# Copying the stack of keys by group of heads, in four bursts of small DMAs with a semaphore each

## The reference, cut to what matters

```python
q = split_heads(query @ Wq.T + bq)      # query: layernorm(x), 16 x 64 x 128
k = split_heads(key @ Wk.T + bk)        # key = value = ctx_1024, 16 x 1601 x 128
v = split_heads(value @ Wv.T + bv)
scores = jnp.einsum('bhqd,bhkd->bhqk', q, k) / np.sqrt(HEAD_DIM)
weights = jax.nn.softmax(scores, axis=-1)
out = jnp.einsum('bhqk,bhkd->bhqd', weights, v)
```

## Time and profile before

| | before |
|---|---|
| median of 3 runs | 583.64 us (582.66 to 584.8) |
| profiled execution, its own time | 585.52 us |
| span of the profiled execution | 583.7 us |
| PE busy | 526.1 us (90%) |
| DVE busy | 418.8 us (72%) |
| ACT busy | 380.7 us (65%) |
| POOL busy | 323.8 us (55%) |
| DMA queue of SP and ACT | 40.09 MB, 39.6% of 16 engines |
| mean granted TensorE clock | 0.970 |

### The profile page before, as it was taken

How to read it: one execution, slowest core, us unless ns; L and a number is a source line. 1 busy time by engine, 2 the same in 40 slices (tenths; PEclk the granted TensorE clock), 3 DMA queues, 4 the chain that set the end, 5 groups by cost and what they waited for, 6 DMA issues and landing times. The chain is left out here.

```text
span 583.7 us, 18814 instructions
## 1 busy us (share of the span) xinstructions
PE 526.1 (90%) x7882; PEld 341.0 (58%) x7882; DVE 418.8 (72%) x749; ACT 380.7 (65%) x704; POOL 323.8 (55%) x197
## 2 busy tenths in 40 slices
PE   2887999999998897999999898999889888999997
PEld 1634555665565464655655565665457565777776
DVE  6187888798797695887887887735887578555554
ACT  4874667677678575776777776976582616656562
POOL 1697968558558456576577279602200024676673
PEclk9887999999999998999999998999999979999999
DMA  7898664674574571754752946101100000000001
GB/s 214 127 131 132 140 104 91 97 117 89 86 116 89 87 108 39 117 105 71 123 106 35 144 84 110 40 2 53 47 2 2 2 1 1 2 2 0 0 0 37
DMA packets 16425, 41.62 MB, mean 71 GB/s; under 512 B 4006, under 2 KB 6830, under 8 KB 16234
## 3 DMA queue, kind: packets, MB, share of 16 engines
q1 hardware_dynamic: 15608, 40.09, 39.6%
q10 hardware_dynamic: 740, 0.42, 0.2%
HBM read 19.70 MB, written 0.52 MB: 35 GB/s over the span
## 5 line engine op out<-in xcount | busy, mean ns | idle before, releaser
L899 DVE TENSOR_REDUCE half_max<-wide 128x2 f32<-128x802 f32 x256 | 241.8, 988 | 57.5 <-PE wide L584 53.6
L824 ACT ACTIVATE probs<-score 128x512 f32<-128x512 f32 (+1 forms) x416 | 225.8, 596 | 75.4 <-PE score L635 75.0
L655 PE MATMUL sums<-probs,values 128*32 128x192 f32 (+3 forms) x3328 | 134.7, 282 | 5.9 <-issue 5.9
L655 PEld LDWEIGHTS sums<-probs,values 128*32 128x32 f32 (+1 forms) x3328 | 87.8, 110 | 60.0 <-issue 31.6
L584 PE MATMUL wide<-k_stack,q_cur 48*128 48x401 bf16 x512 | 88.9, 343 | 13.3 <-ACT k_full L806 6.2
L635 PE MATMUL score<-q_cur,k_stack 50*128 50x128 bf16 (+1 forms) x1664 | 83.4, 219 | 9.6 <-ACT probs L824 5.0
L415 POOL TENSOR_TENSOR ctx_hi<-ctx_in,one 128x1601 bf16<-128x1601 f32 x15 | 42.9, 2860 | 77.3 <-PE wide L506 68.5
L635 PEld LDWEIGHTS score<-q_cur,k_stack 50*128 50x128 bf16 (+1 forms) x1664 | 52.3, 95 | 35.0 <-ACT probs L824 11.3
L1892 POOL TENSOR_TENSOR hid_lo<-hid_e,hid_hi 114x512 bf16<-114x512 f32 x47 | 54.2, 1158 | 32.7 <-ACT hid_hi L1916 31.4
L427 POOL TENSOR_TENSOR k_hi<-k_full,one 128x1601 bf16<-128x1601 f32 x15 | 42.9, 2857 | 43.2 <-ACT k_full L806 34.7
L2027 DVE SCALAR_TENSOR_TENSOR hid_e<-gu,keep_bgu,gate 114x512 f32<-114x512 f32 x48 | 35.9, 750 | 38.5 <-ACT gate L1929 38.3
(11 more groups left out here) (327 smaller groups left out, 923.7 us busy)
## 6 DMA issues: line engine op xcount, KB each, us to landing
k_stack<-k_hi SPq DMA_DIRECT2D x64, 204.0 KB, 6.5
ctx_in<-in_ctx SPq DMA_DIRECT2D x56, 200.1 KB, 3.2
k_stack<-k_lo SPq DMA_DIRECT2D x32, 204.0 KB, 8.7
ctx_in<-in_wgu SPq DMA_DIRECT2D x16, 171.0 KB, 4.9
keep_w<-in_w SPq DMA_DIRECT2D x1, 1368.0 KB
ctx_in<-in_ctx SPq DMA_DIRECT2D x1, 800.5 KB, 8.3
keep_x<-in_x SPq DMA_DIRECT2D x1, 512.0 KB, 6.9
q_cur<-shift SPq DMA_DIRECT2D x30, 2.0 KB
```

Of the source, the lines that this page charges most:

```text
L655: last = pe.matmul(sums[32 * g:32 * g + 32, first * LQ:(first + heads) * LQ], values[0:m, n, k, VW * g + 2 * c:VW * g + 2 * c + 32], probs ...
L824: nc.scalar.activation(probs[0:m, step % NPROB, :].rearrange("r (g p c) -> r p g c", g=G, p=2)[:, p], score[0:m, (2 * step + p) % NSCORE, ...
L899: dve.tensor_reduce(half_max[:, b % 2, :, u // 4, u % 4], wide[:, w, :].rearrange("p (c k) -> p c k", c=2)[:, :, 0:CH], AX.X, ALU.max).the ...
```

## The change

The 6 DMAs of a stack become 24: each of them copies one group, so 16 rows of 1632 elements on both sides, with the source at every fourth partition of a half. For a batch the 6 DMAs of a group stand together. In bodies 1 to 13 the groups are begun at steps 0, 2, 5 and 7 (before: high parts at steps 0 and 1, low parts at step 3). In the prologue and in body 0 no step holds them back; for batch 0 the high parts of all groups come first. Each slot has four semaphores, one a group. PE waits for a group's semaphore at that group's first unit; POOL waits for all four.

```diff
-H_STEP, L_STEP, C_STEPS = 1, 3, (8, 9, 11, 12)
+G_STEPS, C_STEPS = (0, 2, 5, 7), (8, 9, 11, 12)
-        s_stack = [sem(f"s_stack{i}") for i in range(NSLOT)]
+        s_stack = [[sem(f"s_stack{i}_{g}") for g in range(G)] for i in range(NSLOT)]
-        def stacks_of(b):
-
-            return s_stack[b % NSLOT], N_STACK * (b // NSLOT + 1)
+        def stack_lies(e, b, g):
+
+            e.wait_ge(s_stack[b % NSLOT][g], N_STACK * (b // NSLOT + 1))
+            def stack_piece(n, g, term, keys):
+
+                for half in HALVES:
+                    at = half + PAIR * term
+                    sp.dma_start(k_stack[at:at + PAIR, n, g, :], keys[half + g:half + 64:G, :]).then_inc(s_stack[n][g], 16)
+
             def stack(i, b):
-                n, done = b % NSLOT, s_stack[b % NSLOT]
+                n = b % NSLOT
                 if b >= NSLOT:
                     sp.wait_ge(s_score, 2 * NK * (b - NSLOT + 1))
                 if b == 0:
                     sp.wait_ge(s_khi0, 2)
-                else:
-                    sp.wait_ge(s_khi, b)
-                for t in range(2):
-                    if t:
-                        at_step(i, H_STEP)
-                    for half in HALVES:
-                        at = half + PAIR * t
-                        sp.dma_start(k_stack[at:at + PAIR, n, :, :], k_hi[half:half + 64, :]).then_inc(done, 16)
-                at_step(i, L_STEP)
-                if b == 0:
+                    for g in range(G):
+                        for term in range(2):
+                            stack_piece(n, g, term, k_hi)
                     sp.wait_ge(s_klo0, 2)
-                else:
-                    sp.wait_ge(s_klo, b)
-                for half in HALVES:
-                    at = half + PAIR * 2
-                    sp.dma_start(k_stack[at:at + PAIR, n, :, :], k_lo[half:half + 64, :]).then_inc(done, 16)
+                    for g in range(G):
+                        stack_piece(n, g, 2, k_lo)
+                    return
+                sp.wait_ge(s_khi, b)
+                for g in range(G):
+                    if g:
+                        at_step(i, G_STEPS[g])
+                    for term in range(2):
+                        stack_piece(n, g, term, k_hi)
+                    if g == 0:
+                        sp.wait_ge(s_klo, b)
+                    stack_piece(n, g, 2, k_lo)
...
-                pool.wait_ge(*stacks_of(b - 1))
+                for g in range(G):
+                    stack_lies(pool, b - 1, g)
...
+                if part == 0:
+                    stack_lies(pe, b, g)
                 if u == 0:
-                    pe.wait_ge(*stacks_of(b))
                     pe.wait_ge(s_qcur, 2 * (b + 1))
```

## The result

The changed kernel takes 606.01 us (605.05 to 608.63, 4 runs) against 584.22 us (582.66 to 586.09, 4 runs) before: a ratio of 1.0379, 95% interval 1.0332 to 1.0425. The forecast was 579.7 us, faster. The span of the changed kernel is 604.8 us, 21.1 us more.

| | first scores | last scores | loop | after the loop |
|---|---|---|---|---|
| before | 51.77 | 397.64 | 345.9 | 186.1 |
| changed | 59.15 | 416.63 | 357.5 | 188.2 |
| difference | +7.4 | | +11.6 | +2.1 |

A forecast was written before the change was run, and what follows sets the result against it. PE was taken to bound the loop body, busy 20.16 of 21.40 us. Gains of 1.95 us (prologue) and 2.0 (code fetches), the rest at nothing, sum to -3.95 on the median 583.64: 579.7 us, range 572.0 to 586.0.

The forecast's parts named there:

- Issue on SP: SP's queue: 24 issues a stack at 334 ns, 8.0 us; at 654 ns it would be 15.7 us.
- rival D: SP in the prologue: issues at 0.60 to 0.654 us land stack 0 late by 1.7 to 2.9 us; 585.3 to 586.5; chance 0.10.
- Prologue: Start of the kernel: POOL starts 2.7 us earlier, PE's wait ends 1.95 us earlier; gain 1.95 us.
- rival B: Loop and prologue: code stands gone, clock stays up; gain 1.95 + 8 to 14 us, 568 to 574 us; chance 0.19.
- Body, the stack's new places: Main loop: last burst lands by 115.2 us, POOL's `k_hi` at 115.60 just covered, SP not full; cost nothing.
- Waits: PE and POOL: three more waits a batch each; cost 0, at most 2 us.
- Experts' weights: Bodies 12 and 13: their loads now wait for step 7, POOL wants them 10 us later; cost nothing.
- Code fetches: PE's stands in the loop: a fetch costs 1.04 instead of 1.70 us, saving 4.0; half taken, gain 2.0 us.

The follow-up runs named there:

- experiments 2 and 3: Changed kernel, from batch 3 on copies with 16 neighbouring partitions as source (2: 603.97 us) or the same elements read from a buffer in HBM (3: 583.0 us).
- experiment 10: Changed kernel with the four quarters of batch 3's context issued ahead of the stack of batch 1 in the start: 604.1 us, ratio 1.0272.
- old start: Six large copies for batches 0 to 2, as before the change; the run of that name, with 24 small ones from batch 3 on, took 597.0 us.
- experiment 12: Changed kernel with two buffers each for `k_hi` and `k_lo`, so POOL waits for the stack before the last one: 590.23 us, ratio 1.0096.
- the paced kernel: Kernel before the change, its six copies begun at steps 0, 1, 2, 4, 5, 6 instead of 0, 0, 1, 1, 3, 3: 575.75 us, ratio 0.9849.
- new start: Changed kernel with the 24 small copies for batches 0 to 2 alone and six large ones from batch 3 on: 596.71 us, ratio 1.0228.
- burst late: Kernel before the change, its six copies begun two steps later (high parts at step 2, low parts at step 3): 600.23 us, ratio 1.0238.
- experiment 11: The run burst late: kernel before the change with its burst of six copies two steps later, 600.23 us, ratio 1.0238.

## Why the prediction was wrong, by its own steps

**Issue on SP** is the first step that failed, and the others hang on it. But by the prediction's own sums an issue of 0.65 us gives 586.5 us (rival D); the larger part of the 22 us is in the next two steps, priced at nothing. I bounded an issue by 334 and 654 ns and took 334 because both sides of the copy have the same rows. The runs put 589 in its place. At one shape it is 420 ns from HBM and 589 from on-chip memory to on-chip memory (experiments 2 and 3). The row of the old copies, 601 ns, was the nearest by what is copied from where; I chose the row nearest by shape. The 334 was low for HBM too: issued back to back it is 420, and the earlier trace rows had four context loads in 2.03 us. The sums also took the duration of an issue where its pitch counts, which is 43 ns longer.

**Prologue.** Forecast 1.95 us gained, measured 7.4 lost. Rival D had the place and the mechanism and gave 2.9 us at 0.654; POOL's first `k_hi` was 3.06 us late. That the number fits so well is in part luck: the first copy went 0.7 us later than in the profile before, the issues follow each other at 0.63 us, and the last landed after 2.2 us where 3.2 were taken. The other 4.3 us, the shift behind the context loads, I had in no case: I asked when the loads are wanted, not what they meet (experiment 10). The clock in the prologue, which rival B priced at about 4.5 us, is worth some 2 us by the kernels with the old start: first scores at 49.4 and 49.9 us at 1.00, against 51.6 and 51.8 at 0.84.

**Body, the stack's new places.** "At 654 ns a body has 15.7 + 2 + 1.4 us of issues in 21.4: still not full" is true as a sum, and experiment 12 bears it out. It holds for bodies 2 to 11 alone, not for 12 to 14. It left out that longer issues, whose cause no run shows, make 17.9 us of 15.2, and above all that `k_hi` has one buffer: from the last burst over POOL to the first one of the next stack. With all six copies issued by step 3 that ring had 5.5 us of slack in body 2 (the last copy lands at 111.6 us, `k_hi` could be done at 114.5, SP's next stack begins at 120.0); 24 issues in a row, 17.9 us, took it. I looked at POOL's wait once, found it "just covered", and priced a delay by POOL's idle time, though the delay comes back through SP.

**Waits** cost nothing, as forecast: no unit of maxima in the changed kernel waits for a stack. (The bound, 45 times 0.05 us, is 2.3 and not 2.)

**Experts' weights.** Priced at nothing. Bodies 12 to 14 lose 4.1, 2.4 and 3.7 us; in the first two of them these loads stand in SP's queue, and the third waits for the shift behind them; with issues at 420 ns the same bodies take 21.4, 19.0 and 15.8. The prediction asked when POOL wants the loads, not what stands behind them: the shift. So the full queue is the cause, and this is the place where it costs most.

**Code fetches.** Forecast 2.0 us of 9.6 gained, all 9.6 went. The direction was right and the term too small. My reason, that a fetch holds its engine 1.04 instead of 1.70 us, is weak: in the paced kernel fetches are as long as before (1.37 us on average over 98 to 360 us, against 1.36; by the traces' instruction packets) and the stands are gone. The number of copies queued is what the kernels with stands (before, new start, burst late) have in common, six begun within 3.2 to 4.6 us. That a fetch starts late behind them fits the trace: before each of the six stands of the kernel before, the 16 KB packet starts 9.8 to 11.6 us after the one ahead of it, and only one of the other intervals in 98 to 360 us is over 9.5; in the paced kernel one is, 9.9. The wait of a fetch itself no view shows, and experiment 11 does not confirm that the place counts.

The row of the Trainium skill's port map (SBUF — State Buffer, "Door 1: The DMA port swizzle") did bear on the copies. Queued six deep they ran at 122 GB/s with the engines busy to 1.05, so somewhat above the 109 GB/s of the Trainium skill; issued 0.63 us apart they moved 80 GB/s at 0.21:

```profile
61.00:66.00 5.00, 4.10 (x44) 1.83 (x45) 5.00 (x7) 3.26 (x6) 4.92 (x4) 0.50 0.21 80
```

So the engines' time per byte fell to less than a third. This agrees with packets that had queued for few ports, which does not prove it. The Trainium skill's other rule, to coalesce DMAs under 64 KB (DMA: Bandwidth & Descriptors, "Rules for kernel authors"), was right for this kernel: I had rejected it by the landing of transfers, and the price of many small DMAs was paid on the issuing queue.

## What to carry to other kernels

Before cutting a DMA into more, multiply its issue by the count and add it to that queue's whole work for a round; take the price from the row with the same source and destination memory. Do it for the fullest round, not for a typical one: here the rounds with the experts' loads lost most. Then follow every single buffer that the last piece releases round to the queue again, since a piece begun later tightens that ring even where its user has time. If the aim is to keep a queue of transfers short, begin the same few transfers at different steps: six paced copies gave 1.5%, 24 small ones cost 3.8%.

## What the runs showed of the hardware that was not expected

- SP needs 589 ns (median) to issue a copy of 16 x 1632 elements from on-chip memory to on-chip memory and 420 ns for the same from HBM; the bytes (1% of them: 589) and the partition step (589) don't matter. Stores of 128 x 1632 elements from on-chip memory to HBM take 338 and 367 ns. Some issues take 0.8 to 1.3 us longer; why is open.
- A 2 KB DMA on ACT's queue landed some 4 us later when eight loads of SP's queue (1.6 MB) were issued around it than when four of them had gone long before: another issuing queue was no way around them.
- PE's stands for code went from 9.6 us to none by beginning six copies one by one (at most four in flight and not six), with the engines about as busy (0.96 against 1.04) and the fetches as long.
- After waits of 5.0 and 2.5 us PE was granted a clock of 0.85 and 0.74 over the next bodies, and the second was busy for 19.05 us with what took 14.96 at 1.00.
